# The last mixture of experts: outputs gated in expert order and added into the output array by accumulating row scatters

## The reference

```python
logits = t @ switch_w + switch_b                  # t = layernorm(x), 4096 x 128; logits 4096 x 8
route_prob_max = max(softmax(logits), axis=-1)
routes = argmax(softmax(logits), axis=-1)
for e in range(8):
    y = gelu(t @ w1[e] + b1[e]) @ w2[e] + b2[e]    # 128 -> 512 -> 128, tanh approximation of gelu
    out = where((routes == e)[:, None], y, out)
x = x + tanh(g_ffn[3]) * out * route_prob_max[:, None]
```

## Time and profile before

| | |
|---|---|
| time, median of 3 runs | 1066.78 us (1065.4 to 1068.12) |
| profiled execution: span from its first to its last instruction | 1063.2 us |
| busy share of the span | PE 87%, PE weight load 70%, DVE 69%, ACT 60%, POOL 59% |
| chain of work that ended last, by engine | PE 56%, POOL 14%, DVE 11%, issue 9%, ACT 6%, DMA 2% |

### The profile page before, as it was taken

The page is one execution under the profiler, slowest core; times in us unless marked ns, Lnnn a source line. Parts: engine busy times, 40 slices in busy tenths (PEclk is TensorE's granted clock), DMA queues, the critical chain, the costliest instruction groups (busy, mean ns, idle before and its releaser), DMA issues.

```text
span 1063.2 us, 23492 instructions
## 1 busy us (share of the span) xinstructions
PE 920.2 (87%) x8395; PEld 748.4 (70%) x8395; DVE 730.1 (69%) x1618; ACT 640.2 (60%) x1496; POOL 631.6 (59%) x706
## 2 busy tenths in 40 slices
PE   2788888898898998778799899999999988768993
PEld 1566666676898987456676776777777776658993
DVE  6899998363477686578788885555555568836674
ACT  2666776433665666688677776555555566444662
POOL 0467676547772472888777574444444466636753
PEclk9899999999899999899899999999999999868997
DMA  8970000001432341000000000000500000022334
GB/s 237 329 231 2 1 2 2 1 28 52 120 91 60 92 116 41 24 26 24 10 3 1 2 2 2 2 1 2 164 17 2 1 2 2 27 56 62 94 95 146
DMA packets 76852, 57.64 MB, mean 54 GB/s; under 512 B 13603, under 2 KB 69539, under 8 KB 76548
## 3 DMA queue, kind: packets, MB, share of 16 engines
q1 hardware_dynamic: 70148, 42.59, 14.2%
q0 software_dynamic: 6592, 13.58, 4.2%
HBM read 35.30 MB, written 24.08 MB: 56 GB/s over the span
## 4 chain that ended last, share of the span: by engine, by line
PE 56%; POOL 14%; DVE 11%; issue 9%; ACT 6%; DMA 2%; SPq 1%; DVEq 0%; POOLq 0%; ACTq 0%
PE psS L1209 9%; PE psT L1763 6%; PE psO L1827 5%; PE psS L1819 5%; PE psO L1219 5%; PE psS L1219 4%; PE psO L1778 4%; PE psS L1752 3%; POOL sorted_x L1439 3%; POOL ring L847 3%; PE psO L1785 2%; PE psO L1718 2%; PE psM L1739 2%; POOL sorted_z L1452 1%; POOL lnr L890 1%
## 5 line engine op out<-in xcount | busy, mean ns | idle before, releaser
L2152 POOL TENSOR_TENSOR ring<-ring,mx 128x1024 f32<-128x1024 f32 x94 | 178.2, 1903 | 119.4 <-DVE mx L2029 118.7
L1912 ACT ACTIVATE pT<-psT 128x512 f32<-128x512 f32 x192 | 114.3, 595 | 134.1 <-PE psT L1763 134.0
L1266 ACT ACTIVATE pT<-psS,b1copy 128x128 f32<-128x128 f32 x468 | 133.4, 368 | 82.9 <-PE psS L1209 82.9
L1763 PE MATMUL psT<-ident,ring 128*128 128x128 f32 x768 | 125.3, 287 | 26.5 <-POOL ring L2152 14.5
L1209 PE MATMUL psS<-ring 128*128 128x128 f32 x936 | 129.9, 284 | 13.9 <-DVE ring L1324 7.8
L1763 PEld LDWEIGHTS psT<-ident,ring 128*128 128x128 f32 x768 | 88.2, 145 | 67.5 <-issue 35.6
L1209 PEld LDWEIGHTS psS<-ring 128*128 128x128 f32 x936 | 118.7, 199 | 17.1 <-issue 8.2
L2021 DVE TENSOR_TENSOR ring<-psS,bias 128x1024 f32<-128x1024 f32 x96 | 112.9, 1218 | 22.0 <-PE psS L1752 21.4
L2029 DVE TENSOR_REDUCE mx<-ring 128x16 f32<-128x1024 f32 x96 | 112.2, 1209 | 0.0
L1321 DVE COPY ring<-w 128x512 f32 x117 | 54.4, 465 | 56.0 <-PE psO L1219 30.2
L1414 POOL DMA_INDIRECT xrows<-sorted_y,rows x64 | 61.8, 966 | 50.9 <-DMA sorted_y<-pT 33.0
(11 more groups left out here) (304 smaller groups left out, 2105.3 us busy)
## 6 DMA issues: line engine op xcount, KB each, us to landing
w<-w_dram SPq DMA_DIRECT2D x34, 256.0 KB, 6.0
sorted_x<-late SPq DMA_DIRECT2D x18, 256.0 KB, 3.4
ring<-sorted_x SPq DMA_DIRECT2D x18, 256.0 KB, 2.9
sorted_y<-pT SPq DMA_DIRECT2D x17, 256.0 KB, 2.6
sorted_z<-blank_dram SPq DMA_DIRECT2D x2, 1584.0 KB, 9.8
ring<-sorted_z SPq DMA_DIRECT2D x12, 256.0 KB
xrows<-token_y SPq DMA_DIRECT2D x8, 256.0 KB, 3.5
ctxz<-ctxz_dram SPq DMA_DIRECT2D x1, 1056.0 KB, 5.9
```

The lines of the kernel that those rows point to most:

```text
L1266: op = nc.scalar.activation(hs[:, j % 2, f, :], psS[:, j % 2, f * P:(f + 1) * P], func, bias=b1copy[:, j % 4, f:f + 1])
L1763: mm = nc.tensor.transpose(psT[:, i * P:(i + 1) * P], ring[:, u % NS, p * P:(p + 1) * P], ident[:])
L1912: nc.scalar.activation(pT[:, u % 2, 4 * h:4 * h + 4, :].rearrange("p a q -> p (a q)"), psT[:, :], ACT.Exp).then_inc(s_pT, 1)
L2152: nc.gpsimd.tensor_tensor(rows_, rows_, mx[:, u % 4, 0:NH].rearrange("p h -> p h ()").broadcast_to([P, NH, SK]), ALU.subtract).then_inc(s_ ...
```

## The change

The gate is worked out before the rows are sorted and travels with them. `gates` now stands directly ahead of `rank` in both halves; ACT takes t = tanh(d/2) of the difference d, and DVE forms exp(d) = (1 + t) / (1 - t) of all eight experts before it sums. The gate is written into column 129 of the rows that POOL scatters, and the load of the token numbers brings it back in expert order. `outputs` and `output_of_one` multiply each output row by its gate behind the bias. A new use of the semaphore `q.ix` releases PE and the bias copies after the bias sum; `q.ye`, for which POOL waits, comes after the product.

SP stores the residual x to the output half by half as soon as the attention of that half is added (before the first half's sorted rows are loaded, and behind their first two loads). POOL adds the gated rows into the output by indirect DMAs with `compute_op=add`. `token_y`, its eight loads, `combine_last` and the four stores at the end are gone. The output array gets 2 x 3072 rows beyond the tokens for the rows that no token takes; the host cuts them off.

```diff
+ids = sb("ids", [P, 2, LAST_HALF, 2], I32)        # token number and gate, side by side; pwz = the gates
 # last_moe_sync
-    outputs_of(0) behind load 3 of the second half, outputs_of(1) at the end: 2 x 4 loads of token_y
+def residuals_of(h):
+    sp_.wait_ge(s_res, NB - (1 - h) * (B // 2))
+    sp_.dma_start(out[h * HT * P:(h + 1) * HT * P]..., x[:, h * HT:(h + 1) * HT, :]).then_inc(s_out[h], 16)
+residuals_of(0)
 for h in range(2):
     sp_.wait_ge(s_sc[1][h], HT * 16)
     load(h * n); load(h * n + 1); tokens_of(h)      # tokens_of: two columns instead of one
+    if h == 0:
+        residuals_of(1)
     for g in range(2, n): load(h * n + g)
+for k in range(YS):
+    sp_.wait_ge(s_ys[k], scattered(k, 2 * n))
-(end) four waits and stores of x to out
 # route_parts
 choose:     +step(nc.vector.tensor_tensor(pr, pr, over(m), ALU.subtract))        # was the last step of place_rows
+def gates():
+    dve.wait_ge(s_gates[1], h + 1)
+    step(nc.vector.tensor_scalar(tmp, pr, -1.0, 1.0, ALU.mult, ALU.add))
+    step(nc.vector.reciprocal(tmp, tmp))
+    step(nc.vector.scalar_tensor_tensor(tmp, pr, 1.0, tmp, ALU.add, ALU.mult))
+    step(nc.vector.tensor_reduce(sm, tmp, AXX, ALU.add))
+    step(nc.vector.reciprocal(sm, sm))
+    dve.wait_ge(s_token, 2)
+    # one or two steps: rows_low / rows_high[:, tiles, D + 1] = sm * tanh(g)
 # stream: ACT's gates_scalar(act, 0) and DVE's gates() at step 44 (RANK_AT), ahead of rank(); were behind the stream
 # last mixture: ACT's gates_scalar(act, 1) behind the gelu of tile 3; DVE's gates() ahead of outputs(0); were at the end
-nc.scalar.activation(rt3[h][:, 0], rt3[h][:, 0], ACT.Exp)
+nc.scalar.activation(rt3[h][:, 0], rt3[h][:, 0], ACT.Tanh, scale=0.5)
 # outputs(g), r == 1
-nc.vector.tensor_tensor(yslots[...], moe_out[r][...], b2copy[...], ALU.add).then_inc(q.ye.sem, 1)
+nc.vector.tensor_tensor(y, moe_out[r][...], b2copy[...], ALU.add).then_inc(q.ix.sem, 1)
+dve.wait_ge(*q.ix(g + 1)); dve.wait_ge(s_ids[half], 16)
+nc.vector.tensor_tensor(rows_, rows_, pwz[:, half, k:k + n]...broadcast_to([P, n, D]), ALU.mult).then_inc(q.ye.sem, 1)
 # output_of_one: the same with nc.vector.tensor_scalar(y, y, pwz[..., k:k + 1], None, ALU.mult)
 # down(), the waits for a free bank, and copy_weights: q.ye -> q.ix
 # scatter_outputs
+pool.wait_ge(s_out[g // n], 16)                     # once a half
-nc.gpsimd.indirect_dma_start(token_y[g // n], bass.IndirectOffsetOnAxis(ids[:, g // n, k:k + 1], 0), yslots[...], None)
+nc.gpsimd.indirect_dma_start(out, bass.IndirectOffsetOnAxis(ids[:, g // n, k, 0:1], 0), yslots[...], None, compute_op=ALU.add)
```

More of the change, by code:

```diff
@@ L287, in build @@
         s_token, s_ids = sem("tokens_set"), [sem(f"sorted_tokens_loaded{h}") for h in range(2)]
-        s_ys, s_yl = [sem(f"outputs_scattered{k}") for k in range(YS)], [sem(f"outputs_loaded{k}") for k in range(NC // 2)]
+        s_ys = [sem(f"outputs_scattered{k}") for k in range(YS)]
         s_tw = sem("ternary_steps")
         s_ws = sem("ternary_sum")
-        s_out = sem("out")
+        s_out = [sem(f"residuals_stored{h}") for h in range(2)]
         block = ctx.enter_context(nc.Block())
@@ L432, in _ @@
                 last_moe_sync(sp_)
[L433 to L436, removed]
+            for h in range(2):
+                sp_.wait_ge(s_out[h], 16)
         def statistics(n, tile, count):
@@ L1078, in choose @@
                 assert done[0] == CHOSEN
+                step(nc.vector.tensor_tensor(pr, pr, over(m), ALU.subtract))
+                assert done[0] == LOWERED
+            def gates():
[6 more added lines that the diff above has]
+                dve.wait_ge(s_token, 2)
+                at = h * HT
+                for rows_, low, high in ((rows_low, 0, LOW * CH), (rows_high, LOW * CH, NT)):
+                    a, b = max(at, low), min(at + HT, high)
+                    if a < b:
+                        step(nc.vector.tensor_scalar(rows_[:, a - low:b - low, D + 1], sm[:, a - at:b - at], tg[:, LAYERS + 3:LAYERS + 4], None, ALU.mult))
+                assert done[0] == GATED[h]
             def rank():
@@ L1112, in place_rows @@
                 step(nc.vector.tensor_copy(expert[:, h * n:(h + 1) * n], expf[:, h * n:(h + 1) * n]))
[L1113 to L1122, removed]
+            return choose, gates, rank, place_rows
         def gates_scalar(act, h):
-            act.wait_ge(s_half[h], SHIFTED)
-            nc.scalar.activation(rt3[h][:, 0], rt3[h][:, 0], ACT.Exp).then_inc(s_gates[1], 1)
+            act.wait_ge(s_half[h], LOWERED)
+            nc.scalar.activation(rt3[h][:, 0], rt3[h][:, 0], ACT.Tanh, scale=0.5).then_inc(s_gates[1], 1)
         def shared_tensor(pe):
@@ L1281, in moe_scalar @@
                         keep_last(act)
+                    if r and j == GATES_TILE:
+                        gates_scalar(act, 1)
                     if t == 1 and g + 1 < GROUPS[r]:
@@ L1300, in combine, with moe_vector @@
                 statistics(2, c * CH, CH)
[L1302 to L1309, removed]
+        def moe_vector(dve, r, take_last=None, choose_second=None, second_gates=None, rank_second=None, place_second=None):
             l, nch = 3 * r, CHOICES[r]
@@ L1381, in moe_vector @@
                     ahead = j + 1
+                if r and g == 0:
+                    second_gates()
                 outputs(g)
@@ L1384, in moe_vector @@
                     rank_second()
-            if r:
-                second_gates()
-                for cc in range(NC // 2):
-                    combine_last(dve, 1, cc)
         def penalties(pool):
@@ L2101, in stream_vector @@
             dve.wait_ge(s_pen, 8)
-            choose, rank, place_rows, gates = route_parts(dve, 0)
+            choose, gates, rank, place_rows = route_parts(dve, 0)
             for n in range(FIRST, NB + 4):
@@ L2136, in stream_vector @@
                 if n == RANK_AT:
+                    gates()
                     rank()
@@ L2139, in stream_vector @@
                     place_rows()
-                if n == NB + 3:
-                    gates()
             def take_last():
```

79 lines of the change are left out of this document (38 added, 41 removed).

## The result

The changed kernel takes 1084.2 us (median of four runs, 1081.8 to 1087.3), the kernel before beside it on the same chip 1067.5 us (four runs). The ratio is 1.016, 95% interval 1.013 to 1.019: 1.6% slower, where 0.7% faster was forecast. The profiled execution took 1081.82 us, its span is 1080.0.

The account below looks back on a forecast made before the run. PE bounds the last mixture, then a matmul-free tail: 1063.2 - 12.7 (tail) + 4.6 + 0.75 (front, product) + 0.4 (last issues, landing) = 1056.2, -7.0; time 1066.8 - 7.0 = 1060 us, range 1056.5 to 1075.

Parts of the forecast that it names:

- What an accumulating scatter costs POOL: Output scatters of the last mixture: 0.96 us of work, period 1.265 us as for plain ones; upper bound 2.22.
- the sum: Span's end: 1063.2 - 12.7 + 4.6 + 0.75 + 0.4 = 1056.2, a change of -7.0 us.
- Rival A: Last mixture: POOL becomes the bound, slower from a period of 1.64 us; 1071 us at 1.74, 1093 at 2.22; chance 0.28.
- The landing and what follows: Behind the last scatter: landing takes 2.8 us (bounds 2.3 and 4.9), then the span ends; 12.7 us of tail go.
- From span to time: Profiled span is 3.6 us under the runs' median, so forecast time is 1066.8 - 7.0 = 1060 us.
- The front, in the stream: First half's gate steps on DVE ahead of the row sorting: first row scatter 3.0 us later, at 918.4.
- The start of the mixture: Last mixture's first up-projection, released by ACT's evacuation instead of DVE's weight copy: net +1.7 us, near 948.7.
- The second half's gate: DVE's gate steps and product ahead of tile 8's weight copy: 2.4 + 0.75 - 0.33 = +2.9 us; tile 8 near 975.3.
- +4.6: PE from tile 8 on in the last mixture: 1.7 + 2.9 = 4.6 us later, carried to the end.
- ACT's tables (rival D): Second tanh in the last mixture: forecast took no table switch; rival had one, +2.6 us, end 1062.6, chance 0.06.
- SP's queue and the residual stores: Residual stores and doubled token load on SP: hidden behind waits, as is POOL's wait for the stores; zero cost.
- Rival C: Stream and second routing: delays partly caught up, so the front's +4.6 us becomes +2; end 1057.5; chance 0.12.

Follow-up runs that it names:

- after_nogates: Changed kernel without DVE's steps that form the gates (constant 0.5 instead), accumulation kept; 0.986 of the kernel before, on a slower chip.
- after_here: The changed kernel, unchanged, run again on a slower chip; 0.996 of the kernel before there.
- after_padded: Changed kernel with two small, unneeded POOL additions behind each of its 46 accumulating scatters; 1.009 of the kernel before, on a slower chip.
- after_fewer: Changed kernel without the scatter of the fourth tile of each full group (36 scatters, not 46); 0.985 of the kernel before, on a slower chip.
- a_plain: Changed kernel with plain row scatters in place of accumulating ones, residual left out; 1.000 of the kernel before, 1202.8 us on a slower chip.
- a_plain_nogates: Changed kernel with plain scatters and without DVE's steps that form the gates; 0.991 of the kernel before, 1191.5 us on a slower chip.
- before_spread: Kernel before, second half's 16 row scatters sent four at a time behind outputs of groups 0 to 3; 1.014 of the kernel before, 1068.6 us chip.

## Why the prediction was wrong

The step that failed is "What an accumulating scatter costs POOL". It took the plain scatter's 0.96 us and period of 1.265, "since the trace's scatters and gathers ... take the same". They do, but index side against index side says nothing of an added operand. Measured: 1.54 us and 1.85. The bounds, 1.265 to 2.22, held it; the value taken was the lower end. With that the path of the end was wrong too: the sum let group 9's product release the last eleven scatters, while in the changed kernel POOL waited for no product at all.

- *Rival A was the result, and its formula held.* 966.5 + 20.2 + 45 x 1.85 gives a last issue at 1070.0; measured 1072.12, mostly as ten of the 46 scatters took 1.6 to 1.8 us. Its start, 966.5, was measured at 966.76, its threshold of 1.64 was passed. The forecast's last issue was 1053.4: 18.7 of the 23.8 us between 1056.2 and 1080.0 are this.
- *The landing and what follows* are the other 5.1: 3.3 us in place of 2.8, and 4.6 behind it in place of nothing. The sum had taken off all 12.7 us behind the last scatter's landing as if a program ended there. So the range's end at 1075, which stood for rival A at 1.8, was too low by that as well.
- *From span to time:* the 3.6 us added there are not all time ahead of the first and behind the last instruction. In the changed kernel's profiled execution time and span differ by 1.8 us (1081.82 and 1080.0); the rest is the distance from the profiled execution to the median.
- *The front, in the stream:* the first row scatter starts 3.8 us later, predicted 3.0. In the DVE timeline of the changed kernel

```profile
902.13 1.25 DVE L1084 TENSOR_SCALAR ctxz<-ctxz 128x128 f32<-128x128 f32 x1
903.42 0.95 DVE L1085 RECIPROCAL ctxz<-ctxz 128x128 f32<-128x128 f32 x1
...
961.63 0.22 DVE L1084 TENSOR_SCALAR ctxz<-ctxz 128x128 f32<-128x128 f32 x1
```

  the reciprocal takes the 0.95 us that was worked out from 16 and 64 columns, but the step ahead of it took 1.25 us in the stream, beside POOL's shift of the scores (899.54 to 903.30), and 0.22 in the mixture, where POOL was waiting. That one step is the difference; the cause wasn't tested.
- *The start of the mixture:* first up-projection at 949.35, predicted 948.7; released by ACT's evacuation, as said, and no more by DVE's copy.
- *The second half's gate:* tile 8 at 974.77, predicted 975.3. The product of a group took 0.69 us (0.75). The +2.9 is a slip: 2.4 + 0.75 - 0.33 is 2.8.
- *But the front did not reach PE's end.* The sum carried +4.6 through; PE's last down-projection starts 1.2 us later than before. PE in the changed kernel:

```profile
970.07 2.08 PE L1218 MATMUL psS<-ring 128*128 128x128 f32 x8 [4.04 <-DVE ring L1328]
971.93 1.62 PE L1228 MATMUL psS<-ring,pT 128*128 128x128 f32 x8
974.77 1.13 PE L1218 MATMUL psS<-ring 128*128 128x128 f32 x8 [1.22 <-issue]
...
978.42 0.60 PE L1210 MATMUL psT<-ident,ring 128*128 128x128 f32 x4
```

  and before:

```profile
972.50 1.92 PE L1219 MATMUL psS<-ring,pT 128*128 128x128 f32 x8
974.20 1.92 PE L1209 MATMUL psS<-ring 128*128 128x128 f32 x8
975.91 1.46 PE L1219 MATMUL psS<-ring,pT 128*128 128x128 f32 x8
977.21 0.60 PE L1201 MATMUL psT<-ident,ring 128*128 128x128 f32 x4
```

  Windows over the same stretches, first the changed kernel, then before:

```profile
970.07:972.00 1.93, 1.93 (x9) 1.93 (x10) 1.69 (x8) 0.00 (x0) 1.63 (x2) 0.50 0.39 34
974.77:976.00 1.23, 1.23 (x11) 1.23 (x12) 1.03 (x5) 0.06 (x1) 0.93 (x2) 1.00 0.57 53
```

```profile
970.66:974.00 3.34, 3.34 (x16) 3.34 (x17) 2.01 (x8) 1.14 (x4) 2.43 (x4) 0.50 0.15 51
974.00:976.00 2.00, 2.00 (x11) 2.00 (x11) 1.50 (x5) 0.00 (x0) 1.58 (x2) 0.50 0.16 51
```

  Before, the granted clock was 0.50 (1.2 GHz) from 970.66, behind the wait, to 976, and eight matmuls took 2 us: 6.55 us from tile 8's start to the next turn. In the changed kernel it is 0.50 from 970.07, one tile earlier, and 1.00 (2.4 GHz) when tile 8 starts at 974.77: the same work takes 3.65 us. The wait that was forecast near 6 us at tile 8 came as 4.04 us ahead of tile 7 and 1.22 ahead of tile 8. A gap's price is also where its slow restart falls.
- *ACT's tables (rival D):* refuted. Tanh took 0.31 and 0.32 us, and there is no table load beside it.
- *SP's queue and the residual stores:* hidden, as said; POOL never waited for them.
- *Rival C* was right for PE and didn't matter, as POOL's start did not gain from it. Whether the front's us go to the end isn't settled. In after_nogates the output scatters start 10.7 us earlier than in after_here and the span ends 12.0 us earlier, but after_padded and after_fewer, which keep the gates' steps, start theirs 7 and 9 us earlier than after_here as well. By times on one chip, leaving the steps out gave 11 us (a_plain and a_plain_nogates), twice the 5 us that the prediction put on them; on a short chip it wasn't run.

The rule drawn on for rival A, two source reads for an add (the Trainium skill, "Collectives: The Full Stack", section "The bandwidth ceiling: the fold count and why AG ≠ RS ≠ AR"), pointed the right way. The trace does not show a doubling of POOL's work: 1.54 / 0.96 is 1.6.

## What to carry to other kernels

When an engine that merely keeps up gets an operation that the trace doesn't show, work out the period at which its backlog reaches the end, and if the unknown price's bounds straddle that threshold, the forecast is a coin and not the nearest row. Count the work on the issuing engine (46 x 0.59 = 27 us here) against its idle time in the same stretch (9.9 us here), before counting what the receiving side saves. And a change in how densely one engine issues transfers is to be timed on more than one chip.

## What the runs showed of the hardware

- An accumulating indirect DMA of 128 rows costs POOL 1.54 us against 0.96, whether a row has 256 or 512 bytes; back to back they start 1.85 us apart against 1.27, and they land in 3.3 us against 2.3.
- On four of five chips the same kernel took 12.5% longer. Back-to-back plain indirect DMAs (1.27 us apart) left PE with 24 matmuls in 58 us there, against 400; 0.6 us of other POOL work between them brought 239. On the fifth chip, and on the result's, nothing of this is seen (392 matmuls in before_spread, 400 in the kernel before).
- DVE's 128x128 scalar step took 0.22 us beside an idle POOL and 1.25 us beside POOL's shift of 128x1024, one case each.
